# First batch of a two-layer graph attention kernel: order of its loads, of its f columns and chunks of h, engine of the copies out of PSUM, place of the bias additions

## What is computed

```python
# layer 0, for each batch
h = x @ W; f1 = h @ a1; f2 = h @ a2
e = f1 + f2.T; e = where(e >= 0, e, 0.2 * e)
attention = softmax(adj * e, axis=1)
x = attention @ h + bias + x
# layer 1; mean and var are taken over all batches and nodes
support = x @ W1 + b1
y = adj @ support
y = relu((y - mean) * rsqrt(var + 1e-05) * gamma + beta) + x
```

## Time and profile before

| | us |
|---|---|
| median of 3 runs | 943.45 |
| lowest and highest of them | 942.08, 945.23 |
| the profiled execution, its own time | 945.52 |
| its span, first to last instruction | 943.7 |
| PE busy in the span | 885.1 (94%) |
| ACT busy | 800.3 (85%) |
| DVE busy | 715.6 (76%) |
| POOL busy | 293.2 (31%) |

### The profile page before, as it was taken

One profiled execution on the slowest core, in us unless ns is written; L12 is line 12 of the kernel. 1 busy time (PEld: TensorE's weight loads), 2 busy tenths in 40 slices (PEclk: granted clock), 3 DMA queues, 4 the chain that ended last, 5 costly groups with the idle time before them and its releaser, 6 DMA issues.

```text
span 943.7 us, 9327 instructions
## 1 busy us (share of the span) xinstructions
PE 885.1 (94%) x3167; PEld 557.4 (59%) x3167; DVE 715.6 (76%) x789; ACT 800.3 (85%) x619; POOL 293.2 (31%) x390
## 2 busy tenths in 40 slices
PE   7898999999999999999999999999999999999970
PEld 5333656675566756666566756667566666666850
DVE  1654677798678877798778977788777886789966
ACT  4897779997899979998899969999799987997745
POOL 0112241254223442272422641252521633235000
PEclk8999999999999999999999999999999999999995
DMA  8986474867567584766658574765757666565968
GB/s 320 422 342 224 167 274 169 309 224 268 196 241 266 178 321 170 272 248 223 265 217 296 201 307 158 261 242 196 306 189 274 248 224 230 184 232 184 421 285 334
DMA packets 48527, 238.03 MB, mean 252 GB/s; under 512 B 5816, under 2 KB 6440, under 8 KB 23904
## 3 DMA queue, kind: packets, MB, share of 16 engines
q1 hardware_dynamic: 48480, 237.44, 67.4%
HBM read 213.18 MB, written 24.23 MB: 252 GB/s over the span
## 4 chain that ended last, share of the span: by engine, by line
PE 79%; POOL 5%; DMA 4%; DVE 4%; issue 4%; ACT 1%; SPq 1%; DVEq 0%; ACTq 0%; POOLq 0%
PE acc L512 34%; PE acc L481 11%; PE acc L483 11%; PE acc L487 10%; PE acc L469 4%; DMA adj_slot<-adjT 3%; PE acc L493 3%; PE acc L446 3%; DVE scores L728 2%; POOL hz_lo L881 2%; POOL hz L866 2%; POOL hz_hi L878 2%; PE acc L525 1%; PE acc L528 1%; PE acc L527 1%
## 5 line engine op out<-in xcount | busy, mean ns | idle before, releaser
L749 DVE TENSOR_TENSOR exp_lo<-scores,hi 128x2048 fp32r<-128x2048 f32 (+1 forms) x133 | 273.9, 2072 | 123.7 <-ACT hi L622 123.4
L728 DVE CUSTOM_DVE_ANT_0 scores<-scores,adj_slot 128x2048 f32<-128x2048 f32 x128 | 298.8, 2334 | 50.2 <-ACT scores L601 21.6
L608 ACT ACTIVATE scores<-scores,neg_mx 128x2048 f32<-128x2048 f32 x128 | 255.8, 1998 | 26.9 <-DVE neg_mx L731 26.9
L622 ACT CAST hi<-scores 128x2048 fp32r<-128x2048 f32 (+1 forms) x133 | 214.9, 1631 | 63.1 <-PE acc L487 59.0
L601 ACT ACTIVATE scores<-adj_slot,f_cols 128x2048 f32<-128x2048 f32 x128 | 255.8, 2004 | 9.8 <-issue 5.2
L512 PE MATMUL acc<-adj_slot,region_even 128*128 128x512 f32 x512 | 228.7, 592 | 0.0
L512 PE MATMUL acc<-adj_slot,region_odd 128*128 128x512 f32 x392 | 175.3, 592 | 0.8 <-DVE region_odd L782 0.8
L481 PE MATMUL acc<-hi,hz_lo 128*128 128x512 f32 x448 | 161.1, 482 | 13.6 <-POOL hz_lo L881 13.6
L512 PEld LDWEIGHTS acc<-adj_slot,region_even 128*128 128x128 f32 x512 | 96.8, 190 | 100.0 <-issue 95.8
L481 PEld LDWEIGHTS acc<-hi,hz_lo 128*128 128x128 f32 x448 | 85.0, 191 | 73.8 <-issue 43.5
L483 PE MATMUL acc<-hi,hz_hi 128*128 128x512 f32 x448 | 124.8, 402 | 0.0
(11 more groups left out here) (76 smaller groups left out, 600.9 us busy)
## 6 DMA issues: line engine op xcount, KB each, us to landing
adj_slot<-adjT SPq DMA_DIRECT2D x151, 1024.0 KB, 4.9
adj_slot<-xT SPq DMA_DIRECT2D x12, 1024.0 KB, 9.8
adj_slot<-biasT SPq DMA_DIRECT2D x32, 256.0 KB, 6.4
xp_dram<-adj_slot SPq DMA_DIRECT2D x32, 256.0 KB, 2.5
adj_slot<-xp_dram SPq DMA_DIRECT2D x8, 1024.0 KB, 9.0
adj_slot<-f_rows SPq DMA_DIRECT2D x7, 1024.0 KB, 7.1
adj_slot<-y_dram SPq DMA_DIRECT2D x7, 1024.0 KB, 9.2
outT<-adj_slot SPq DMA_DIRECT2D x6, 1024.0 KB, 5.5
```

What stands on the lines that cost most here:

```text
L608: act.activation(scores[e][:, :], scores[e][:, :], ACT.Exp, bias=neg_mx[:, e:e + 1], accum_out=zsum[:, e:e + 1]).then_inc(exp_done, 1)
L622: act.copy(hi[m][:, part_cols(t, i)], scores[e][:, part_cols(t, i)]).then_inc(hi_done, 1)
L728: dve.tensor_tensor_reduce(scores[e][:, :], scores[e][:, :], slots[s][:, :], 1.0, NEG_BIG, ALU.mult, ALU.max, mx[:, e:e + 1]).then_inc(max ...
L749: dve.tensor_tensor(exp_lo[e][:, part_cols(t, i)], scores[e][:, part_cols(t, i)], hi[m][:, part_cols(t, i)].bitcast(F32), ALU.subtract).th ...
```

## The change

All of it lies in the first batch and its start.

- **Loads at the start.** SP loads adjacency tile 1 directly behind tile 0. The loads of x for batches 1 to 7 are spread behind later tiles (`X_AFTER`: behind the load of tile 1, 3, 4, 5, 7, 8, 9), and `rows_of_f` stands ahead of tiles 1, 2, 3, 4, 6, 7, 9 in place of 0, 0, 1, 3, 5, 7, 8. W1, b1, gamma and beta are loaded behind the last adjacency tile; the waits for them stand at the first support chunk.
- **f columns and h.** Two column pairs come first, so that the edge scores of tiles 0 and 1 need no others. PE then makes chunk 0 of h into `acc0[0]`, the other 14 column pairs, and chunks 1 to 3 of h into `acc1[1..3]` (`h0_banks`).
- **Copies out of PSUM.** DVE copies h (`first_h`: chunk 0 ahead of score(1), chunks 1 to 3 behind recip(0), recip(1), recip(2)) and the rows of f (`rows_from_psum`, behind recip(10)); ACT did both. Layer 0 waits for the copy of h for bank `acc0[0]` alone.
- **End of the batch.** POOL's four bias additions stand behind all 16 scalings. `load_f1` stands ahead of the bias and the four loads of x.

```diff
--- before.py
+++ after.py
@@ -88,7 +88,8 @@
-    F_STEP = {1: 0, 2: 0, 3: 1, 4: 3, 5: 5, 6: 7, 7: 8}
+    X_AFTER = {1: 1, 2: 3, 3: 4, 4: 5, 5: 7, 6: 8, 7: 9}
+    F_STEP = {1: 1, 2: 2, 3: 3, 4: 4, 5: 6, 6: 7, 7: 9}
     ROWS_STEP, TURN_STEP = F_STEP[B - 1] + 1, NT - 2
@@ -148,6 +149,7 @@
         acc1 = [ctx.enter_context(nc.psum_tensor(f"acc1_{c}", [P, CH], F32)) for c in range(NC)]
+        h0_banks = [acc0[0]] + acc1[1:]
@@ -324,15 +326,20 @@
                 if is_first(bt):
-                    sp.dma_start(x1_sb[:, :], xT[1]).then_inc(x1_loaded, 16)
                     for t in range(1, NT):
-                        for b in X_STAGE:
-                            if max(F_STEP[b], 1) == t:
-                                load_x(b, X_STAGE[b])
                         if t in STAGED:
...
                         load_adj(bt, t)
+                        for b in X_AFTER:
+                            if X_AFTER[b] == t and b == 1:
+                                sp.dma_start(x1_sb[:, :], xT[1]).then_inc(x1_loaded, 16)
+                            elif X_AFTER[b] == t:
+                                load_x(b, X_STAGE[b])
+                    sp.dma_start(w1_sb[:, :], W1).then_inc(w1_loaded, 16)
+                    sp.dma_start(b1_sb[:, :], b1.partition_broadcast(P)).then_inc(b1_loaded, 16)
+                    sp.dma_start(gb[:, 0:1], gamma).then_inc(gb_loaded, 16)
+                    sp.dma_start(gb[:, 1:2], beta).then_inc(gb_loaded, 16)
@@ -342,11 +349,10 @@
                     load_adj(nx, 1)
+                    load_f1(nx)
                     load_bias(bt)
-                    for c in range(NC - 1):
+                    for c in range(NC):
                         load_residual(bt, c)
-                    load_f1(nx)
-                    load_residual(bt, NC - 1)
                 else:
@@ -388,10 +394,6 @@
             load_adj(Batch(0, 0, 0), 0)
-            sp.dma_start(w1_sb[:, :], W1).then_inc(w1_loaded, 16)
-            sp.dma_start(b1_sb[:, :], b1.partition_broadcast(P)).then_inc(b1_loaded, 16)
-            sp.dma_start(gb[:, 0:1], gamma).then_inc(gb_loaded, 16)
-            sp.dma_start(gb[:, 1:2], beta).then_inc(gb_loaded, 16)
             steps(sp, step)
@@ -449,7 +451,10 @@
                 if t == 0 and is_first(bt):
-                    pe.wait_ge(h_out, c + 1)
+                    if c == 0:
+                        pe.wait_ge(h_out, 1)
+                    else:
+                        pe.wait_ge(f1_out, c + 1)
                 elif t == 0:
@@ -489,6 +494,8 @@
                 pe.wait_ge(xp_done, NC * bt.n + c + 1)
+                if is_first(bt) and c == 0:
+                    pe.wait_ge(w1_loaded, 16)
                 for q in range(TC):
@@ -568,15 +575,16 @@
                 if c == 0:
-                    f_columns([0], acc1[3])
+                    f_columns([0, 1], acc1[3])
                 pe.matmul(acc0[c][:, :], wa1_cols, x0_sb[:, cols(c)], start=True, stop=True)\
                     .then_inc(f1_mm, 1)
-            f_columns(range(1, NT), acc1[0])
             pe.wait_ge(w_loaded, 16)
-            for c in range(NC):
-                pe.wait_ge(f1_out, c + 1)
-                make_h(Batch(0, 0, 0), x0_sb, acc0, c)
-            pe.wait_ge(w1_loaded, 16)
+            pe.wait_ge(f1_out, 1)
+            make_h(Batch(0, 0, 0), x0_sb, h0_banks, 0)
+            f_columns(range(2, NT), acc1[0])
+            pe.wait_ge(f_out, 1)
+            for c in range(1, NC):
+                make_h(Batch(0, 0, 0), x0_sb, h0_banks, c)
             steps(pe, step)
@@ -595,7 +603,7 @@
                     act.wait_ge(f_out, 3)
-                if t == 1 and is_first(bt):
+                if t == 2 and is_first(bt):
                     act.wait_ge(f_out, 2)
@@ -640,8 +648,8 @@
-            def h_from_psum(bt, banks, chunks=range(NC)):
-                for c in chunks:
+            def h_from_psum(bt, banks):
+                for c in range(NC):
                     act.wait_ge(h_mm, NC * bt.n + c + 1)
@@ -662,15 +670,10 @@
                         y_from_psum(bt.prev())
-                    if t == 0 and is_first(bt):
-                        h_from_psum(bt, acc0, [2, 3])
                     if t > 0 and not is_first(bt):
...
                         edge(bt, t + 2)
-                    if is_first(bt) and t == ROWS_STEP:
-                        act.wait_ge(f_mm, rows_done(B - 1))
-                        act.copy(f_sb, acc1[0][:, :]).then_inc(row_out, 1)
                 if not is_last(bt):
@@ -685,7 +688,6 @@
             edge(first, 1)
-            h_from_psum(first, acc0, [0, 1])
             steps(act, step)
@@ -718,6 +720,14 @@
+            def rows_from_psum():
+                dve.wait_ge(f_mm, rows_done(B - 1))
+                dve.tensor_copy(f_sb, acc1[0][:, :]).then_inc(row_out, 1)
+
+            def first_h(c):
+                dve.wait_ge(h_mm, c + 1)
+                dve.tensor_copy(region[0][:, cols(c)], h0_banks[c][:, :]).then_inc(h_out, 1)
+
             def score(bt, t):
@@ -779,6 +789,8 @@
                 dve.wait_ge(sup_mm, NC * bt.n + c + 1)
+                if is_first(bt) and c == 0:
+                    dve.wait_ge(b1_loaded, 16)
                 dve.tensor_tensor(region[bt.par][:, cols(c)].rearrange("p (t f) -> p t f", f=P),
@@ -790,6 +802,10 @@
                         recip(bt, t)
+                    if is_first(bt) and t + 1 < NC:
+                        first_h(t + 1)
+                    if is_first(bt) and t == ROWS_STEP:
+                        rows_from_psum()
                     if is_first(bt) and t == TURN_STEP:
@@ -815,18 +831,19 @@
             dve.wait_ge(f_mm, 1)
-            dve.tensor_copy(f2_cols[:, 0, 0:1], acc1[3][:, FA2:FA2 + 1]).then_inc(f_out, 1)
-            dve.wait_ge(f_mm, 2)
-            dve.tensor_copy(f2_cols[:, 0, 1:NT],
-                            acc1[0][:, 0:2 * NT].rearrange("p (t k) -> p t k", k=2)[:, 1:NT, FA2]).then_inc(f_out, 1)
+            dve.tensor_copy(f2_cols[:, 0, 0:2],
+                            acc1[3][:, 0:4].rearrange("p (t k) -> p t k", k=2)[:, :, FA2]).then_inc(f_out, 1)
...
             dve.tensor_copy(own[:, :, B - 1], wa_sb[:, FA2:FA2 + 1].to_broadcast([P, B - 1])).then_inc(wa_out, 1)
-            dve.wait_ge(b1_loaded, 16)
             score(Batch(0, 0, 0), 0)
+            dve.wait_ge(f_mm, 2)
+            dve.tensor_copy(f2_cols[:, 0, 2:NT],
+                            acc1[0][:, 0:2 * NT].rearrange("p (t k) -> p t k", k=2)[:, 2:NT, FA2]).then_inc(f_out, 1)
+            first_h(0)
             steps(dve, step)
@@ -890,12 +907,12 @@
                     scale_h(bt, t)
-                    if t == 12:
+                    if t == 12 and not is_first(bt):
                         add_bias(bt, 0)
-                    if t == 14:
+                    if t == 14 and not is_first(bt):
                         add_bias(bt, 1)
-                add_bias(bt, 2)
-                add_bias(bt, 3)
+                for c in range(0 if is_first(bt) else 2, NC):
+                    add_bias(bt, c)
```

## The result

The changed kernel takes 933.17 us, median of four runs (931.71 to 934.28), against 944.34 us for the kernel before on the same chip: a ratio of 0.988 with a 95% interval of 0.986 to 0.991. The forecast was 931.4 us, range 929.0 to 936.5. Of the some 1.8 us between them, 0.9 lie in the kernel before, whose median was 943.45 for the forecast, and 0.8 in the saving, 11.2 in place of 12.0.

What follows compares the result with a forecast made beforehand. PE, busy 94% of the span, was taken to bound the kernel. Start 4.7, clock 1.3, stall 6.0 and seam 0 sum to 12.0 us off the 943.45 us median: 931.4 us, range 929.0 to 936.5.

Steps and rivals of the forecast that it cites:

- When PE is free: First batch, ahead of tile 0: PE would be done with its earlier work between 22.0 and 22.8 us.
- When tile 0 is ready: First batch: DVE's inversion at 21.4 and POOL's scaling would have tile 0 ready at 21.9 us, perhaps 1 us later.
- The clock at tile 0: First batch: tile 0 would lose little to PE's lower clock, a gain of 1.3 us, ends 0 and 1.74.
- signs that I had named as wrong: Trace signs against the forecast, among them PE idle ahead of tile 0 with POOL or a load as releaser.
- The row groups: Two row-matmul groups (1.92 us) leave the hole ahead of tile 0 for PE's solid stretch; one group costs 1.0 there.
- The stall: PE's 4.09 us wait ahead of tile 13 and the slow tile's 1.88 us would both go, 5.97 us.
- The seam: Between layer 0 and layer 1 of the first batch: PE would not wait, 2.1 us to spare; 2.7 us kept as risk.
- The second batch: No-change case: DVE and POOL meet in another order there and give most back, about 943 us; chance 0.03.
- the late first tile: Rival at the start: tile 0 starts at 24.3 to 24.6 and runs slowly, 934.5 us; chance 0.15.
- the held seam: Rival between layers 0 and 1: loads or additions come 2 to 5 us late, 933.5 to 937 us; chance 0.15.
- the slower row copy: Rival late in layer 0: DVE's copy of the rows comes so late that the kernel slows, 948 us; chance 0.02.
- That ACT holds layer 0: Rival in layer 0: ACT, not PE, sets the pace, so only the stall's 6 us remain, 937.5 us; chance 0.05.

Runs made afterwards that it cites:

- run 1: The kernel before with only POOL's four bias additions of the first batch moved behind all scalings: 938.35 us, ratio 0.992.
- run 3: The changed kernel with x of batches 1 to 7 loaded in the old order, batches 1 to 3 ahead of adjacency tile 1: 934.81 us, ratio 0.989.
- run 4: The changed kernel with all start loads in the old order, W1, b1, gamma and beta again behind adjacency tile 0: 936.39 us, ratio 0.991.
- Run 2: The changed kernel with POOL's bias additions of the first batch back at their old places, behind tiles 12 and 14: 943.72 us, ratio 0.998.
- run 5: The changed kernel with the next f1 row loaded behind the bias and three pieces of x: 933.10 us, ratio 0.986.
- run 11: The changed kernel with the f rows copied out of PSUM on ACT behind the edge scores of tile 12, a single execution: 928.24 us.
- run 12: The changed kernel with the f rows copied on ACT behind the edge scores of tile 12, timed in six executions: 932.29 us, ratio 0.986.
- run 9: The changed kernel with the first group of row matmuls ahead of tile 0 and h chunk 0 copied by ACT: 929.55 us, ratio 0.983.

## Why the prediction was right

**When PE is free:** wrong by 3 us, harmless for when tile 0 starts, not for its clock. I put it at 22.0 to 22.8 and it was 19.06 (21.45 less 2.39). I had let one chunk of h run at the upper clock; all ran there, 24 records in 2.92 us where 32 took 6.64 in the earlier trace rows. The profile of before was one case of the clock: in run 1, with that same order, h took 3.82.

**When tile 0 is ready:** 21.35 against my 21.9. The DVE copy took 0.60 start to start (0.67 to 0.68 recorded) against the 0.65 taken. I bound the start to PE instead, 22.6, so this term gave 7.8 us rather than 6.6. That tile 1's load held tile 0 in the kernel before was right: runs 1, 3 and 4. I left out a term here, the four small loads taken from the front, which run 4 prices at 2.05 us. Tile 1 landed at 13.5 (issued at 4.49, 9.0 us to landing) where I had 16.5; it does not show, since DVE came to this tile only at 18.32.

**The clock at tile 0: the step that failed.** I took 1.3 us and got 0: 5.23 us as before. I had read from the earlier trace rows that the clock falls only behind the idle time, and not seen that my own sum leaves PE an idle time whenever it is free early. This is one of the signs that I had named as wrong: PE was idle for 2.39 us ahead of tile 0, until POOL's scaling at 20.95 was done. Of six profiles with this order ahead of tile 0 (the changed kernel twice, runs 2, 5, 11 and 12), one had it fast, run 11, in which the clock had been at the lower level during h (24 records in 4.43 us), the wait was 0.89 us, and the clock was up again at tile 0.

**The row groups:** two more in the solid stretch at 1.0 us each, as taken from the group at 34.37. Another 0.3 us came with them, since a tile between two groups takes 3.63 us and not 3.49.

**The stall:** 5.97 us taken, and the arithmetic closes with it. From tile 0's start to the end of layer 0 it was 68.8 us before and 65.2 now: 3.6 us less, and 6.0 - 2.0 - 0.3 = 3.7. The additions alone gave 5.5 in S. But I added it up as a term that stands by itself, and it is so only one way. Run 2 shows that the gain at the start passes through the wait ahead of tile 13 only if the additions move too. My working would have given that kernel 937.5 us; it takes 943.7.

**The seam:** no wait, as forecast. In the changed profile the last sum ends at 90.57 (89.88 + 0.69) and PE wants it at 92.9 (the support's start at 90.2 and three chunks of 0.89): 2.3 us to spare where I had 2.1. The four small loads took SP 1.85 us to issue in place of 2.4 (SP's timeline, for the earlier trace rows):

```profile
64.23 0.43 SPq L342 DMA_DIRECT2D gb<-beta  x1
...
69.42 0.90 SPq L284 DMA_DIRECT2D adj_slot<-adjT  x2
70.36 0.43 SPq L319 DMA_DIRECT2D adj_slot<-f_rows  x1
```

The two tiles were issued at 69.42, in the 68.5 to 70.3 of the forecast. The f1 row's place is what keeps it: run 5.

**The sum:** 7.8 + 0 - 2.0 - 0.3 + 6.0 = 11.5 against 11.4 in S. The forecast was 6.6 - 1.9 + 1.3 + 6.0 = 12.0: the start 1.2 too small, the clock 1.3 too large, the groups 0.4 too cheap. That the first two nearly cancel is luck, though both come from PE being free 3 us sooner than I thought. The second batch gave nothing back. Of the rivals, the late first tile, the held seam, and the slower row copy did not occur (the copy began at 62.6). That ACT holds layer 0 was wrong for this kernel, and also one step further: in run 9 it is a load, with POOL beside DVE, that PE waits for, ahead of ACT, which I had called the next limit.

## What to carry to other kernels

- A gain ahead of a wait that ends with a transfer is swallowed unless the transfer comes earlier too or the wait is moved. Ask what the transfer itself stands behind: here it was a copy that the change had put one tile later. So two edits in a row can be worth 11.4 us together with -1.4 and 5.5 each alone; price each against the other's absence.
- Before a difference under half a per cent is explained, cut the trace at a repeated point and look at the distances: here they come in two sizes, 1.6 us apart, and seven of them account for some 3 us between two profiles of nearly the same kernel.

## What the runs showed of the hardware

- **The granted clock differs from profile to profile for the same instructions.** The eight f1 records took from 5.16 to 6.72 us in the kernels with the changed start, 32 of h 3.82 or 6.64. At the start of the later batches, 98 idle times of 1.8 to 2.2 us on PE were followed by a clock that fell in 66 cases and stayed up in 32. Ahead of tile 0, where the idle time of the new order ran from 0 to 6.3 us, the tile was fast behind each of up to 1.85 us and slow behind each from 2.39 us on.
- **Small loads cost far more than their bytes.** Four of 129 KB together held the 1 MB loads behind them back by 2.05 us, seen at the multiplication of tile 1 in run 4 against run 3.
- **A copy out of PSUM on VectorE leaves POOL alone.** POOL's scaling at 20.95 took 0.40 us with that copy at 20.78 to 21.45 beside it, where the one at 26.68 in the earlier trace rows took 2.5 beside a multiplication, and the one at 57.36 in run 9 took 2.52. This agrees with the Trainium skill, "SBUF — State Buffer", section "SBUF: two separate sides", by which POOL is shut out only by VectorE operations that use both SBUF ports or read two tensors from SBUF. The copy itself took 0.67 to 0.68 us on VectorE and 0.56 to 0.59 on ScalarE. An estimate from the section "The TRN2 errata" of "VectorE: DVE Perf Modes" in the Trainium skill gives 658 and 570 ns, and the trace agrees.
